# Two layer norms centred by ScalarE, accumulating negated means, and a new order of every queue in a four-layer graph kernel

## The reference, cut to what matters

```python
h = jnp.maximum(_layernorm(x, axis=-1), 0.0)
x = x + _L0_gnn_ref(h, adj, ...)   # hypergraph convolution 256->512, ReLU, layer norm, 512->256, + h
h = jnp.maximum(_layernorm(x, axis=-1), 0.0)
x = x + _L1_gnn_ref(h, adj, ...)   # graph attention, softmax over nodes, ELU
h = jnp.maximum(_layernorm(x, axis=-1), 0.0)
x = x + _L2_gnn_ref(h, adj, ...)   # three powers of a normalised transition matrix, ReLU
h = jnp.maximum(_layernorm(x, axis=-1), 0.0)
x = x + _L3_gnn_ref(h, adj, ...)   # attention scores masked by adj, summed, softmax over nodes, times values
```

## Time and profile before

| | |
|---|---|
| runs | 1441.32, 1443.7 and 1443.85 us, median 1443.7 |
| profiled execution | 1441.33 us, span 1439.5 us |
| TensorE | busy 1381.0 us (96%) |
| weight loads | busy 1246.3 us (87%) |
| VectorE | busy 1286.3 us (89%) |
| ScalarE | busy 1056.8 us (73%) |
| GpSimd | busy 948.3 us (66%) |
| granted TensorE clock, mean | 0.984 |

### The profile page before, as it was taken

One profiled execution on the slowest core, in us unless ns is written; L12 is line 12 of the kernel. 1 busy time (PEld: TensorE's weight loads), 2 busy tenths in 40 slices (PEclk: granted clock), 3 DMA queues, 4 the chain that ended last, 5 costly groups with the idle time before them and its releaser, 6 DMA issues.

```text
span 1439.5 us, 33470 instructions
## 1 busy us (share of the span) xinstructions
PE 1381.0 (96%) x8924; PEld 1246.3 (87%) x8924; DVE 1286.3 (89%) x5197; ACT 1056.8 (73%) x2345; POOL 948.3 (66%) x974
## 2 busy tenths in 40 slices
PE   7499999999999999999999999999999999999985
PEld 5378998998998899999889899989989988989975
DVE  6669999999999999999999999999999999999883
ACT  4267788777778777777877777887777788777764
POOL 4466666677666667666667766666776666676533
PEclk9699999999999999999999999999999999999997
DMA  4001011011111011111101111110111110111001
GB/s 125 30 16 38 23 52 48 28 45 51 37 51 51 29 44 44 51 36 51 51 22 44 51 49 39 51 43 30 44 51 36 51 51 22 44 50 36 30 31 51
DMA packets 75382, 62.14 MB, mean 43 GB/s; under 512 B 3013, under 2 KB 70985, under 8 KB 75338
## 3 DMA queue, kind: packets, MB, share of 16 engines
q1 hardware_dynamic: 75338, 61.63, 13.5%
HBM read 36.45 MB, written 16.78 MB: 37 GB/s over the span
## 4 chain that ended last, share of the span: by engine, by line
PE 69%; DVE 19%; issue 6%; POOL 3%; ACT 1%; DVEq 0%; POOLq 0%; DMA 0%; ACTq 0%
PE ps L357 30%; PE ps L342 19%; PE ps L361 15%; DVE stats L1316 4%; DVE z L1455 3%; PE ps L418 2%; DVE prod L1499 2%; POOL rs L1038 2%; PE ps L463 2%; DVE x L1462 2%; DVE zb L1428 1%; DVE h L1328 1%; DVE mv L1321 1%; DVE nmean L1335 1%; POOL var_e L1036 1%
## 5 line engine op out<-in xcount | busy, mean ns | idle before, releaser
L1096 POOL TENSOR_TENSOR x3n<-p,x 128x512 f32<-128x512 f32 x64 | 82.3, 1286 | 255.7 <-ACT p L851 255.7
L1058 POOL TENSOR_TENSOR hT_lo<-hT,hT_hi 128x512 fp32r<-128x512 f32 x126 | 161.1, 1301 | 73.1 <-ACT hT L793 42.2
L1038 POOL TENSOR_TENSOR rs<-var_e,neg_half 128x4 f32<-128x4 f32 x160 | 165.0, 1031 | 23.7
L772 ACT ACTIVATE p<-ps,rs 128x256 f32<-128x256 f32 (+1 forms) x256 | 136.1, 595 | 28.0 <-DVE sij L1416 27.7
L357 PE MATMUL ps<-wl_hi,h2T_hi 128*128 128x512 f32 (+1 forms) x512 | 148.8, 372 | 0.9 <-DVE x L1462 0.8
L342 PE MATMUL ps<-p,alT 128*128 128x256 f32 (+1 forms) x512 | 147.1, 386 | 0.5 <-DVE p L1440 0.5
L357 PE MATMUL ps<-wl_lo,h2T_hi 128*128 128x512 f32 (+1 forms) x512 | 132.3, 340 | 0.0
L361 PE MATMUL ps<-wl_hi,h2T_lo 128*128 128x512 f32 (+1 forms) x512 | 132.1, 339 | 0.0
L1316 DVE BATCH_NORM_STATS2 stats<-x 128x6 f32<-128x256 f32 x256 | 108.7, 425 | 5.9 <-issue 0.2
L869 ACT ACTIVATE h3T_hi<-ps 128x512 fp32r<-128x512 f32 x64 | 38.3, 598 | 89.4 <-PE ps L463 86.9
L793 ACT ACTIVATE hT_hi<-ps,cols_sb 128x512 fp32r<-128x512 f32 x128 | 87.4, 683 | 21.6 <-PE ps L361 21.6
(11 more groups left out here) (186 smaller groups left out, 4622.6 us busy)
## 6 DMA issues: line engine op xcount, KB each, us to landing
x_in<-in_x SPq DMA_DIRECT2D x32, 512.0 KB, 3.4
out_x<-x SPq DMA_DIRECT2D x32, 512.0 KB, 3.2
adj_f<-in_adjT SPq DMA_DIRECT2D x32, 256.0 KB, 2.7
adj_m<-in_adjT SPq DMA_DIRECT2D x32, 256.0 KB, 2.8
adj_l<-adj_m SPq DMA_DIRECT2D x32, 256.0 KB, 2.3
vqk<-in_l_wk SPq DMA_DIRECT2D x3, 256.0 KB, 4.8
x<-in_w1T SPq DMA_DIRECT2D x1, 512.0 KB, 6.0
x<-in_w2T SPq DMA_DIRECT2D x1, 512.0 KB, 6.9
```

The lines of the kernel that those rows point to most:

```text
L772: return act.activation(dst, src, ACT.Copy, scale=scale)
L1038: pool.tensor_tensor(rs[:, layer, :], var_e[:, layer, :], neg_half[:], ALU.pow).then_inc(done, G)
L1058: pool.tensor_tensor(hTs[1][:, hc, :], hT[:, hc, :], hTs[0][:, hc, :], ALU.subtract).then_inc(S["hT_lo"], 1)
L1096: pool.tensor_tensor(x3n[:, s], p0[:, s], x2[:, s], ALU.add).then_inc(S["x3_ready"], 2)
```

## The change

1. For layers 2 and 3 VectorE writes negated means (`spread_about`, now with `accum_out`), and ScalarE subtracts them with ReLU (`mid_centre`, `late_centre`); `centred` is no longer called. The negated mean of layer 1 and `first_scale` get the accumulating form too.
2. The bank table and the order of all engines' `body` are new, with the waits that belong to them. Among others: `next_d` goes behind `mid_p10(3)`; all `front_w1` come first in a round; two of the four `front_att`, and `late_ak` and all `mid_az`, move into the round before; exp, elu and layer 2's moments move from a round's end to the next one's start.
3. `first` and `opening` have a new order too.

```diff
@@ spread_about (VectorE)
-                dve.tensor_scalar(nmean[:, layer, gs], mv[:, layer, gs, 0], -1.0, None, ALU.mult).then_inc(done, 2)
+                dve.tensor_scalar(nmean[:, layer, gs], mv[:, layer, gs, 0], -1.0, None, ALU.mult, ALU.add,
+                                  accum_out=unread[:, layer, b:b + 1]).then_inc(done, 2)
@@ first_scale (VectorE)
                     dve.tensor_scalar(w2c[:, c, :], raw_w2[:, c, :], cols_sb[:, 1, c:c + 1], None,
-                                      ALU.mult).then_inc(S["w2_scaled"], 1)
+                                      ALU.mult, ALU.add, accum_out=unread[:, 5, c:c + 1]).then_inc(S["w2_scaled"], 1)
@@ mid_ln2, late_ln3 (VectorE)
-                centred(2, x2, h, b, r.mid, S["st2"], S["ag2"], S["h2_ready"])
+                spread_about(2, x2, b, r.mid, S["st2"], S["ag2"], S["nm2_ready"])
...
-                centred(3, x3n, h, b, r.late, S["st3"], S["ag3"], S["h3_ready"])
+                spread_about(3, x3n, b, r.late, S["st3"], S["ag3"], S["nm3_ready"])
@@ new on ScalarE
+            def mid_centre(r, b):
+                centre(2, x2, h, b, r.mid, S["nm2_ready"], S["h2_ready"])
+
+            def late_centre(r, b):
+                centre(3, x3n, h, b, r.late, S["nm3_ready"], S["h3_ready"])
@@ waits of next_d and mid_ap (TensorE)
             def next_d(r):
-                wait(pe, S["dots_ready"], r.front(2))
...
             def mid_ap(r, g):
                 if g == 0:
+                    wait(pe, S["dots_ready"], r.front(2))
@@ body of ScalarE, its start
                 if r.has_front:
                     copy_u(r, 0)
-                if past.has_front:
-                    elu_exp(past, 0)
-                if past.has_mid:
-                    relu_p0(past, 1)
+                    copy_u(r, 1)
+                    copy_u(r, 2)
+                    copy_u(r, 3)
+                if r.has_mid:
+                    mid_centre(r, 0)
                 if past.has_front:
                     elu_exp(past, 1)
...
@@ opening of ScalarE
                 copy_u(r, 2)
+                copy_u(r, 3)
                 square(r, 0)
-                copy_u(r, 3)
...
-                copy_yT(r, 0)
                 leaky_part(r, 0)
                 leaky_part(r, 1)
                 softmax(r, 0)
                 softmax(r, 1)
+                copy_yT(r, 0)
+                copy_yT(r, 1)
@@ opening of VectorE, its end
+                y_low(r, 0)
+                y_low(r, 1)
                 front_low(r, 0)
                 front_low(r, 1)
                 second_dots()
-                y_low(r, 0)
-                y_low(r, 1)
                 elu_low(r, 0)
-                elu_high(r, 0)
-                elu_low(r, 1)
-                later1 = r.later(1)
-                mid_ln2(later1, 0)
-                elu_high(r, 1)
-                mid_ln2(later1, 1)
-                mid_low(later1, 0)
@@ first of VectorE
-                first_scale()
                 y_low(r, 0)
                 y_low(r, 1)
+                first_scale()
```

More of the change, by code:

```diff
@@ L472, in mid_p2 @@
                     wait(pe, S["h2T_lo"], r.mid(G))
+                elif g == 3:
+                    wait(pe, S["wex_ready"], r.tail(G))
                 pe.wait_ge(S["h2T_copied"], r.mid(2 * (g // 2) + 2))
@@ L510, in front_w2 @@
                     pe.wait_ge(S["w2_ready"], 3)
[L511 to L514, removed]
+                if g == 3:
+                    if not r.steady and r.i == 0:
+                        wait(pe, S["hT_ready"], r.front(G))
                 pe.wait_ge(S["hT_hi"], r.front(G))
@@ L530, in mid_ap @@
                 if g == 0:
+                    wait(pe, S["dots_ready"], r.front(2))
+                    if not r.steady and r.i == GROUPS:
+                        wait(pe, S["wcol_ready"], r.tail(G))
+                elif g == 1:
                     if not r.steady and r.i == 1:
-                        wait(pe, S["deg_ready"], r.next(G))
-                elif g == 1:
-                    wait(pe, S["p10_copied"], r.mid(3))
+                        wait(pe, S["p10_copied"], r.mid(3))
+                elif g == 2:
+                    wait(pe, S["vqk_copied"], r.late(1))
                 elif g == 3:
@@ L545, in late_vqk @@
                 if g == 0:
-                    wait(pe, S["deg_ready"], r.next(G))
+                    if not r.steady and r.i == GROUPS:
+                        wait(pe, S["zb_ready"], r.mid(G))
                 elif g == 1:
-                    if not r.steady and r.i in (GROUPS, GROUPS + 1,):
-                        wait(pe, S["wcol_ready"], r.tail(G))
+                    wait(pe, S["p10_copied"], r.mid(G))
+                elif g == 2:
+                    wait(pe, S["gt_ready"], r.next(G))
                 elif g == 3:
                     wait(pe, S["lz"], r.front(2))
-                    if not r.steady and r.i == GROUPS:
-                        wait(pe, S["p10_copied"], r.mid(G))
                 pe.wait_ge(S["h3T_copied"], r.late(2 * (g // 2) + 2))
@@ L583, in front_b1 @@
             def front_b1(r):
-                wait(pe, S["p10_copied"], r.mid(G))
-                wait(pe, S["vqk_copied"], r.late(1))
                 pe.wait_ge(S["wh12_ready"], r.front(G))
@@ L602, in late_ak @@
             def late_ak(r):
-                wait(pe, S["hT_hi"], r.next(1))
                 pe.wait_ge(S["vqk_copied"], r.late(G))
@@ L775, in copy_vqk @@
                 if g == 0:
-                    wait(act, S["vw_ready"], r.tail(2))
+                    if not r.steady and r.i in (GROUPS - 1, GROUPS, GROUPS + 1,):
+                        wait(act, S["vw_ready"], r.tail(2))
                 elif g == 2:
-                    if not r.steady and r.i in (GROUPS, GROUPS + 1,):
-                        wait(act, S["vw_ready"], r.tail(G))
+                    wait(act, S["vw_ready"], r.tail(G))
                 act.wait_ge(S["rs3_ready"], r.late(G))
@@ L830, in keep_x3 @@
             def keep_x3(r):
-                wait(act, S["x4_ready"], r.tail(2))
                 wait(act, S["x4_ready"], r.tail(G))
+                if not r.steady and r.i in (GROUPS, GROUPS + 1,):
+                    wait(act, S["x4_ready"], r.tail(2))
                 act.wait_ge(S["x3_ready"], r.late(G))
@@ L1578, in body @@
             def body(r):
+                past = r.later(-1)
                 ahead = r.later(1)
```

328 lines of the change are left out of this document (173 added, 155 removed), and 6 rows, old and new, of the table BANK.

## The result

The changed kernel took 1428.47, 1430.59 and 1430.6 us (median 1430.59) against a median of 1443.7: ratio 0.9909, 95% interval 0.9887 to 0.9932. That is 13.1 us less, where 23.7 were forecast. The profiled execution took 1430.59 us with a span of 1428.8.

What follows compares the result with a forecast made beforehand. TensorE was taken to bound the kernel, with about 0.6 us of small waits a round. From 1441.3 us, head −12.3, steady rounds −10 and tail −0.5 gave 1418.5, forecast as 1420, range 1406 to 1436.

Steps and rivals of the forecast that it cites:

- The bound and its room: Steady rounds: TensorE bounds them at 42.36 us each, with about 0.6 of small waits, 17.4 us at most.
- The negated mean: VectorE, ahead of the dots: the accumulating form does not wait for GpSimd, 0.7 us less a round, bounds 0 and 0.78.
- Order: Steady rounds: spread of the degrees no longer waits for dots; 0.6 us of waits go, 0.25 come: −10, bounds 0 and −17.4.
- rival (a): Steady rounds: gain cancelled, waits move to the h2 transposes or the negated mean stays blocked; 1428.5 us, chance 0.22.
- Subtraction to ScalarE: Layers 2 and 3, per round: VectorE −3.1 us, ScalarE +4.0, neither the bound; way to transposes 0.1 to 0.2 longer if free.
- Rival (d): Steady rounds: slower, ScalarE's layer 2 subtraction comes behind a 128x512 activation; 0.75 us more a round, 1450 us, chance 0.10.
- Head: Opening and round 1: round 2 starts 12.3 us earlier, bounds −8 and −15.
- step 5: Round 1: its waits go, but its fourth `front_w1` waits about 2 us for a bank; net −0.6 us.
- Steps 2 and 4: Opening: 2, spread of wh at 48.0 instead of 53.93, −5.9 us; 4, `y_low` ahead of second dots, −3.4.
- step 1: Opening: `y_low` goes first, `front_w1` starts at 17.1 instead of 18.83: −1.7 us, −0.5 more from a moved square.
- step 3: Opening: the first leaky part goes ahead of a copy of yT that waited for TensorE: −1.05 us.
- Tail: Last rounds: moments without subtractions give 0.8 to 1.0 us, the round before pays 0.5: −0.5, bounds −2 and +1.5.

Runs made afterwards that it cites:

- experiment 1: Changed kernel with wh formed by four accumulating 128x2 instructions instead of one 128x8 product: 1412.95 us, ratio 0.98.
- experiment 2: Changed kernel with GpSimd's first sum p+bk of a round made to wait for wh: 1413.38 us, ratio 0.9804.
- experiment 4: Kernel before the change with only the accumulating form of the negated mean added: 1428.8 us, ratio 0.9912.
- experiment 5: Version of experiment 2 with GpSimd's wide low parts back ahead of the opening's last inverse root: 1415.25 us, ratio 0.982.
- experiment 6: Version of experiment 2 with `y_low` back behind the second dots in the opening: 1417.74 us, ratio 0.983.
- experiment 7: Version of experiment 2 with `first_scale` in its plain form and back ahead of `y_low`: 1415.94 us, ratio 0.9824.
- experiment 10: Version of experiment 4, in the old order, with the part of the new opening that needs no other banks: 1416.08 us, ratio 0.9811.
- experiment 11: Version of experiment 2 with GpSimd's wide low parts in the opening also waiting for wh: 1411.3 us, ratio 0.9785.
- experiment 12: Version of experiment 11 with 25 unused identity products in TensorE's early idle time: 1411.46 us, ratio 0.9783.
- experiment 3: Changed kernel with plain negated means for layers 1 to 3, `first_scale` still accumulating: 1443.95 us, ratio 1.0017.
- experiment 9: Version of experiment 4, in the old order, with ScalarE subtracting the means of layers 2 and 3: 1443.42 us, ratio 1.0005.
- experiment 8: Version of experiment 2 with VectorE subtracting the means of layers 2 and 3 again, without their negated means: 1440.04 us, ratio 0.9987.

## Why the prediction was right in sign and off in size

**The bound and its room.** Right, and a little too large. A steady round had about 0.5 us of waits that the list did not name: without them it takes 41.85 or 41.87 us in nine versions (experiments 1, 2, 4 to 7 and 10 to 12), where I had 42.36 less 0.6.

**The negated mean.** Right, and the heart of the matter: 154 to 158 ns in 192 executions, experiments 3 and 4. The Trainium skill, "SBUF — State Buffer", section on the two separate sides, gives whichever starts first the shared ports for the whole instruction, and names VectorE instructions with two SBUF inputs beside the two-port modes. The trace agrees with both halves: wh is held 1.24 us when it comes 0.06 us behind the sum, and in round 3, where it starts 0.12 us ahead of the second sum, it takes 0.19 and ends 0.02 us behind the first.

**Order, the step that failed.** "I put 0.25 us of new waits a round against 0.6 that go: 0.35 × 29 = −10 us." Measured +0.65. The first product over alT indeed waits for no dots (slack 0.4 held, experiments 1 and 2), and the h2 transposes wait once, for 0.2 us. What I left out is the instruction behind the dots: wh, on VectorE, against a GpSimd queue in which the first of the two `add_bias` had moved behind `front_scale1`, next to the second. I had seen wh held in the opening (1.17 us) and allowed for it there as a bound, but did not ask where GpSimd's sums would stand when the dots of a steady round come 1 us earlier. It costs 42.45 − 41.87 = 0.58 us in a round of the loop. Over the 29 rounds experiment 2 takes 1329.11 − 115.05 = 1214.06 us where the changed kernel takes 1348.65 − 118.92 = 1229.73, so 15.7 come back there: with wh free, the rounds would have gained 15 us, more than the 10 forecast. This is rival (a) in its size (1428.5 against 1430.6), by a mechanism that it does not name: that the time lies in the stated range is owed to the room left for that rival, not to the account of the rounds.

**Subtraction to ScalarE.** "Neither becomes the bound" was right; that its way to the transposes costs 0.1 to 0.2 us if ScalarE is free, and more behind a 128x512 activation, was right for the old order as far as the activation goes (experiment 9: 0.40 a round); the 0.1 to 0.2 was not measured alone. Rival (d) did not occur in the new order. That VectorE's relief is needed there (experiment 8, 0.9 a round) I had not seen.

**Head.** Forecast −12.3 at round 2, measured −12.8, and that these lie so near is in part luck. By steps: `front_w1` at 17.1, measured 16.45; dots at 47.3, measured 44.85 (44.77 + 0.08); the spread of wh at 48.0, measured 46.24 with wh held for 1.19; round 1 at 59.9, measured 57.26. TensorE and VectorE in the changed opening, in place of the earlier trace rows:

```profile
16.45 0.70 PE L357 MATMUL ps<-yT_hi,w_hi 128*128 128x512 f32 x2 [0.54 <-DVE yT_lo L1235]
...
46.24 1.11 PE L414 MATMUL ps<-ident,wh 128*128 128x128 f32 x4 [2.95 <-DVE wh L1527]
...
57.26 0.62 PE L357 MATMUL ps<-yT_hi,w_hi 128*128 128x512 f32 x2
```

```profile
44.99 1.19 DVE L1527 TENSOR_TENSOR wh<-wh12r,rs 128x8 f32<-128x8 f32 x1
```

Round 1 came earlier than forecast and then took 44.55 us, so step 5's −0.6 was wrong in sign. Two things that I had at most in the bounds, not in the sum, work against each other. The clock of this execution's opening gave some 3 us up to the first sum of squares (last section): where it was the lower one, in experiments 5, 6 and 8, `front_w1` started at 17.03 to 17.04 us, as forecast. And the held wh took some back: between the first sums of squares of rounds 1 and 2 the kernel before takes 40.69 us, the changed kernel 42.78 and experiment 2 40.53. In that stretch round 1's wh lasts 0.91 us instead of 0.17, and the granted clock of round 1 is 0.92 instead of 1.00 in experiment 2; how much is the stall and how much the clock behind it was not separated. Steps 2 and 4 are borne out singly by the traces of experiments 5 and 6; step 1 by the start of `front_w1` in experiment 7, while its share of the time stays open; step 3 was not tried alone.

**Tail.** Forecast −0.5, measured +1.5. The wait of the earlier trace rows did not shrink, and round 32, for which I had 0.5, has one of 2.97 us, since both pairs of h2 transposes now share a bank and the second waits for VectorE's low part of the first:

```profile
1381.59 1.12 PE L465 MATMUL ps<-ident,h 128*128 128x128 f32 x4 [2.97 <-DVE h2T_lo L1239]
...
1407.69 1.09 PE L465 MATMUL ps<-ident,h 128*128 128x128 f32 x4 [2.05 <-ACT h L885]
```

About half of the loss goes with wh once more: in round 31 it lasts 0.90 us and stands on the chain that ends last, and from that round's first sum of squares to the end experiments 1 and 2 take 79.3 and 79.5 us, where the changed kernel takes 80.2 and the kernel before 78.7. How much of the rest is the bank and how much the chain ahead of it was not tried.

## What to carry to other kernels

When a shorter chain brings an instruction forward, look up what the other engines do at its new moment, above all for VectorE instructions with two SBUF inputs beside GpSimd: here the stall did not go, it moved to the next instruction that can be held. The remedy is either a form that is not held or a wait that puts GpSimd behind. And try the smallest edit alone first: here another form of one small instruction in the old order gave what the new order of five queues gave.

## What the runs showed of the hardware

Whether a VectorE instruction of 128x8 takes 0.19 or 1.24 us was decided by a start 0.12 us ahead of or 0.06 us behind that of GpSimd's second sum: it ended 0.02 us behind the sum during which it started, here and in experiment 4 (732.89 + 0.23 = 733.12, the sum at 731.82 + 1.28 = 733.10). Accumulating forms of 128x2 took 206 to 218 ns (with a scalar per partition) and 154 to 158 ns (with a constant) whatever GpSimd did.

Plain instructions of 128x256 in `first_scale` took 341 to 1354 ns, accumulating ones in the changed kernel 472 to 478.

TensorE's clock in the opening differs between executions. In the profiled ones of the changed kernel and of experiments 1, 2 and 11 two passes of the first `front_w1` take 0.70 us; in those of experiments 3, 5, 6 and 8, with the same program up to there, 1.22. Experiment 5:

```profile
17.04 1.22 PE L357 MATMUL ps<-yT_hi,w_hi 128*128 128x512 f32 x2
```

The granted clock reads 1.00 there in all of them, so I read the level from the passes: 1.22 us is what the same two took at 70.14 in the kernel before, where the granted clock was 0.50, the lower level of 1.2 GHz. Round 0's first sum of squares came at 31.0 to 31.2 in the former, at 33.1 in experiment 3 and at 34.1 to 34.3 in the other three. The runs without a trace may be of either kind (those of experiment 5 lie at 1414.8 to 1415.3 and at 1418.6 to 1418.8), so differences of 2 or 3 us between medians, as between experiments 2, 5, 7 and 11, are not firm. What decides it was not found; experiment 12 did not settle it.
